# Five hand-ordered engine programs of a linear-attention and MoE layer are written out anew, with another table of PSUM banks

## What is computed

```
x = x + attention(layernorm(x)):   q = elu(x Wq') + 1, k = elu(x Wk') + 1, v = x Wv'  (16 heads of 16)
    out_i = q_i . sum_{j<=i} k_j v_j' / (q_i . sum_{j<=i} k_j + 1e-8), then out Wo'
x = x + ffn(layernorm(x)):         8 experts of 256 -> 128 -> 256 (silu(x Wg) * (x Wu)) Wd, weighted by
    a router (sigmoid, bias, best 2 of 4 groups, best 4 of 8 experts), and one shared expert without weight
```

## Time and profile before

| | |
|---|---|
| median of three runs | 1032.64 us |
| the profiled execution | 1031.95 us, of which its span (first to last instruction) is 1030.2 us |
| PE, DVE busy | 1007.4 us (98%), 838.3 us (81%) |
| POOL, ACT busy | 537.6 us (52%), 422.3 us (41%) |
| DMA | 96.48 MB, 94 GB/s in the mean |

### The profile page before, as it was taken

One profiled execution on the slowest core, in us unless ns is written; L12 is line 12 of the kernel. 1 busy time (PEld: TensorE's weight loads), 2 busy tenths in 40 slices (PEclk: granted clock), 3 DMA queues, 4 the chain that ended last, 5 costly groups with the idle time before them and its releaser, 6 DMA issues.

```text
span 1030.2 us, 22106 instructions
## 1 busy us (share of the span) xinstructions
PE 1007.4 (98%) x8437; PEld 859.6 (83%) x8437; DVE 838.3 (81%) x1776; ACT 422.3 (41%) x750; POOL 537.6 (52%) x440
## 2 busy tenths in 40 slices
PE   6889999999999999999999999999999999999997
PEld 5768888888888888888888888888888888888886
DVE  4888888888978889898788978889888888977554
ACT  5754343434434344343434434344343434422222
POOL 5864545556354463545556345463545556343643
PEclk9999999999999999999999999999999999999999
DMA  5011425345252543425345253444424345231321
GB/s 204 3 47 57 104 63 137 66 117 110 62 144 60 137 83 105 109 58 139 67 114 111 59 142 70 135 83 104 107 64 136 66 121 114 59 107 58 102 82 42
DMA packets 235160, 96.48 MB, mean 94 GB/s; under 512 B 161712, under 2 KB 217520, under 8 KB 235056
## 3 DMA queue, kind: packets, MB, share of 16 engines
q1 hardware_dynamic: 235056, 95.07, 36.1%
HBM read 66.60 MB, written 28.44 MB: 92 GB/s over the span
## 4 chain that ended last, share of the span: by engine, by line
PE 90%; DVE 3%; ACT 2%; DMA 2%; issue 1%; POOL 1%; SPq 0%; DVEq 0%; ACTq 0%; POOLq 0%
PE bank L997 55%; PE y_bank L997 19%; PE bank L1106 6%; PE bank L1122 5%; PE bank L1093 2%; PE bank L1136 2%; PE bank L1148 1%; DMA cw_all<-in_w_qkvo 1%; DMA x_dram<-blocks 0%; DMA cw_all<-cw_dram 0%; DMA expo<-x_dram 0%; ACT wg_hi L580 0%; DVE et L965 0%; DVE x_mid L990 0%; ACT expo L641 0%
## 5 line engine op out<-in xcount | busy, mean ns | idle before, releaser
L997 PE MATMUL bank<-xt_hi,wg_hi 128*128 128x512 f32 x576 | 237.4, 412 | 3.0 <-DVE et L965 2.3
L746 POOL TENSOR_TENSOR h_lo<-et,h_hi 128x512 fp32r<-128x512 f32 x142 | 180.9, 1290 | 96.6 <-ACT h_hi L696 96.4
L997 PE MATMUL bank<-xt_lo,wg_hi 128*128 128x512 f32 x576 | 228.5, 397 | 0.0
L997 PE MATMUL bank<-xt_hi,wg_lo 128*128 128x512 f32 x576 | 228.5, 397 | 0.0
L743 POOL TENSOR_TENSOR et<-et,cw_all 128x512 f32<-128x512 f32 x124 | 163.5, 1339 | 115.1 <-DVE et L971 97.6
L871 DVE TENSOR_TENSOR scores<-bank,cst 128x512 f32<-128x512 f32 x240 | 152.6, 681 | 41.4 <-PE bank L1106 34.1
L997 PE MATMUL y_bank<-wd_hi,h_hi 128*128 128x256 f32 x576 | 165.0, 286 | 0.3 <-POOL h_lo L746 0.3
L997 PE MATMUL y_bank<-wd_hi,h_lo 128*128 128x256 f32 x576 | 161.5, 280 | 0.0
L997 PE MATMUL y_bank<-wd_lo,h_hi 128*128 128x256 f32 x576 | 161.4, 280 | 0.0
L997 PEld LDWEIGHTS bank<-xt_hi,wg_hi 128*128 128x128 f32 x576 | 108.6, 189 | 40.5 <-issue 16.8
L965 DVE SCALAR_TENSOR_TENSOR et<-et,bank 128x512 f32<-128x512 f32 x144 | 95.9, 677 | 48.7 <-ACT et L687 48.6
(11 more groups left out here) (131 smaller groups left out, 1830.5 us busy)
## 6 DMA issues: line engine op xcount, KB each, us to landing
...
```

What stands on the lines that cost most here:

```text
L746: nc.gpsimd.tensor_tensor(h_lo[:, i % HR, :], et[:, i % ET, :], h_hi[:, i % HR, :].bitcast(f32), ALU.subtract).then_inc(h_lo_done, 1)
L997: ins = nc.tensor.matmul(dst, l, r, start=first and n == 0, stop=last and n == 2, skip_group_check=shared)
```

## The change

Every list in `FIRST`, `STEP` and `LAST` is another order of the same parts with the same work; each list is also cut at another place, so that `STEP` begins elsewhere in the cycle. `BANK` has other banks for some parts. ACT's order of pieces is no longer 0 to 9, so those who wait for a high half now look up its place in ACT's list; the first masks wait for the one piece that is staged where they write, where they waited for piece 5; the first `cw_load` waits for pieces 8 and 9, where it waited for 9.

```diff
 STEP = { "PE": """
-        ... values.0.1 values.1.1 down.5.3 inter.0.1 inter.1.1 scores.3.1 gate.0.2 router.0.2 values.2.1
-        values.3.1 gate.1.2 up.0.2 inter.2.1 inter.3.1 gate.2.2 k.0.0 q.0.0 k.1.0 up.2.2 down.6.3 up.1.2
-        q.1.0 down.7.3 down.8.3 scores.0.0 up.4.2 v.1.0 v.0.0 gate.4.2 gate.5.2 state.0.0 ...
+        ... values.0.1 values.1.1 down.3.3 inter.1.1 scores.3.1 gate.0.2 router.0.2 values.2.1 values.3.1
+        gate.1.2 gate.2.2 up.0.2 inter.2.1 down.7.3 inter.3.1 down.6.3 inter.0.1 k.0.0 q.0.0 k.1.0 up.2.2
+        v.1.0 up.1.2 q.1.0 scores.0.0 down.8.3 v.0.0 gate.5.2 gate.3.2 up.3.2 gate.4.2 state.0.0 ...
 FIRST = { "PE": """
-        turn.0.0 turn.1.0 warm.17.0 v.1.0 k.0.0 q.0.0 v.0.0 k.1.0 q.1.0 scores.0.0 k_turn.0.0 scores.1.0
-        warm.8.0 turn.0.1 turn.1.1 ...
+        warm.8.0 turn.1.0 turn.0.0 warm.17.0 k.0.0 q.0.0 v.1.0 k.1.0 q.1.0 v.0.0 scores.0.0 scores.1.0
+        k_turn.0.0 turn.0.1 turn.1.1 ...
     "ACT": """
-        piece.0.0 piece.1.0 turn.1.0 turn.0.0 piece.2.0 v.1.0 piece.3.0 k.0.0 piece.4.0 piece.5.0 q.0.0 ...
+        piece.4.0 piece.1.0 piece.0.0 turn.1.0 turn.0.0 piece.3.0 piece.2.0 k.0.0 q.0.0 piece.5.0 ...
     "SP": """
-        load_x.0.0 consts.0.0 piece.0.0 piece.1.0 piece.2.0 load_x.0.1 piece.3.0 ...
+        load_x.0.0 piece.4.0 piece.1.0 piece.0.0 consts.0.0 piece.2.0 piece.3.0 load_x.0.1 ...
 LAST = { "ACT": """
-        ... gate.3.15 split.2.15 split.3.15 gate.4.15 gate.5.15 ...
+        ... gate.3.15 split.2.15 gate.4.15 gate.5.15 split.3.15 ...
     "SP": """
-        ... cw_store.0.15 cw_load.0.15 cw_load.1.15 cw_load.2.15 store.0.14 cw_load.4.15 cw_load.3.15 ...
+        ... cw_store.0.15 cw_load.2.15 cw_load.0.15 cw_load.5.15 cw_load.1.15 cw_load.7.15 cw_load.6.15
+        cw_load.3.15 store.0.14 cw_load.4.15 store.0.15
 BANK = {
-    ... ("gate", 8): 3, ("router", 0): 1, ("turn", 1): 5, ("up", 8): 5, ...
+    ... ("gate", 8): 5, ("router", 0): 5, ("turn", 1): 1, ("up", 8): 3, ...
@@
-        split_hi = sem("split_hi")
+        split_hi, SPLIT_HI = sem("split_hi"), nth("ACT", ("piece",))
@@ cw_load, on SP
                     if b == 0:
-                        wait_split(sp, NP - 1)
+                        for n in range(NS, NP):
+                            wait_split(sp, n)
@@ mask, on ACT and likewise on DVE
                     if b == 0:
-                        wait_split(act, KC + 3)
+                        wait_split(act, KC + (i % SM) // 2)
@@ piece, on POOL and likewise on DVE
-                    pool.wait_ge(split_hi, i + 1)
+                    pool.wait_ge(split_hi, SPLIT_HI["piece", i, 0])
```

More of the change, by code:

```diff
@@ L40 @@
+        inter.1.1 scores.3.1 gate.0.2 router.0.2 values.2.1 values.3.1 gate.1.2 gate.2.2 up.0.2 inter.2.1
+        down.7.3 inter.3.1 down.6.3 inter.0.1 k.0.0 q.0.0 k.1.0 up.2.2 v.1.0 up.1.2 q.1.0 scores.0.0
+        down.8.3 v.0.0 gate.5.2 gate.3.2 up.3.2 gate.4.2 state.0.0 up.4.2 wo.0.1 up.5.2 wo.1.1 down.0.2
+        scores.1.0 down.1.2 down.2.2 gate.6.2 gate.8.2
         """,
     "ACT": """
-        split.5.3 split.3.3 split.4.3 gate.8.3 gate.7.3 wide.1.1 gate.6.3 ln1_apply.0.0 take.2.2 take.3.2
@@ L51 @@
+        weigh.5.2 weigh.3.2 rstd2.0.1 weigh.4.2 split.3.2
         """,
     "DVE": """
[L53 to L56 removed]
@@ L59 @@
+        den.1.0 at.1.1 state.0.0 gate.4.2 gate.5.2 gate.3.2 up.3.2 up.5.2 up.4.2 wo.1.1 wo.0.1 ln2_stats.0.1
+        mask.4.0 mask.6.0 ln2_apply.0.1 blocks.1.1 mask.5.0 mask.7.0 ln1_stats.0.-1 gate.6.2
         """,
     "SP": """
-        load_x.0.0 put.1.2 get.1.2 put.0.0 get.0.0 cw_store.0.2 cw_load.1.2 cw_load.0.2 put.2.0 get.2.0
-        cw_load.2.2 cw_load.3.2 store.0.3 cw_load.4.2 cw_load.6.2 cw_load.7.2 cw_load.5.2
+        cw_load.7.3 cw_load.6.3 cw_load.5.3 get.1.2 put.0.0 get.0.0 cw_store.0.2 cw_load.1.2 cw_load.0.2
@@ L63 @@
+        put.2.0 cw_load.4.2 get.2.0 store.0.3 cw_load.3.2 cw_load.2.2 load_x.0.-1 put.1.1
         """,
@@ L66 @@
     "PE": """
-        turn.0.0 turn.1.0 warm.17.0 v.1.0 k.0.0 q.0.0 v.0.0 k.1.0 q.1.0 scores.0.0 k_turn.0.0 scores.1.0
-        warm.8.0 turn.0.1 turn.1.1 k_turn.1.0 state.0.0 values.0.0 scores.2.0 inter.0.0 values.1.0 scores.3.0
-        k.0.1 q.0.1 inter.1.0 state.1.0 values.2.0 values.3.0 q.1.1 inter.2.0 scores.0.1 inter.3.0 warm.10.0
-        k.1.1 wo.0.0 wo.1.0 scores.1.1 k_turn.1.1 v.1.1 v.0.1 k_turn.0.1 values.0.1 state.0.1 scores.2.1
-        state.1.1 turn.3.0 inter.0.1 turn.2.0 inter.1.1 values.1.1 scores.3.1 gate.1.0 router.0.0 gate.0.0
@@ new lines @@
+        k.1.1 wo.0.0 wo.1.0 scores.1.1 k_turn.0.1 v.1.1 k_turn.1.1 v.0.1 state.0.1 values.0.1 scores.2.1
+        turn.2.0 inter.1.1 turn.3.0 inter.0.1 values.1.1 state.1.1 warm.10.0 scores.3.1 gate.0.0 gate.1.0
+        turn.1.2 turn.0.2 gate.2.0 router.0.0 values.2.1 values.3.1 inter.3.1 k.0.2 q.0.2 k.1.2 up.0.0
+        inter.2.1 q.1.2 k_turn.0.2 v.1.2 up.1.0 v.0.2 down.0.0 scores.0.2 up.2.0 gate.3.0 gate.4.0 state.0.2
+        k_turn.1.2 gate.5.0 up.4.0 wo.1.1 wo.0.1 up.3.0 up.5.0 down.1.0 scores.1.2 gate.6.0 down.2.0
@@ L136 @@
+        split.7.14 split.8.14 split.6.14 weigh.2.15 weigh.0.15 weigh.1.15 split.0.15 split.1.15 split.2.15
+        weigh.3.15 weigh.4.15 weigh.5.15 split.4.15 split.5.15 split.3.15 split.6.15
         """,
     "DVE": """
[L138 to L140 removed]
@@ L146 @@
-        weigh.6.15 gate.8.15 up.8.15 split.7.15 split.8.15 result.0.15
+        gate.8.13 gate.7.13 state.1.15 up.7.13 up.6.13 up.8.13 mask.11.15 mask.10.15 mask.9.15 mask.8.15
+        mask.12.15 mask.13.15 mask.14.15 mask.15.15 router.0.14 spread.1.15 route.0.14 rank0.0.14 rank1.0.14
+        mult.1.15 gate.0.14 spread.0.15 up.0.14 result.0.13 mult.0.15 gate.2.14 at.1.15 at.0.15 up.2.14
+        gate.3.14 gate.1.14 wo.0.15 up.1.14 wo.1.15 ln2_stats.0.15 up.3.14 ln2_apply.0.15 blocks.1.15
+        gate.4.14 up.4.14 gate.5.14 up.5.14 gate.8.14 gate.6.14 gate.7.14 up.8.14 up.7.14 up.6.14
@@ L147 @@
+        router.0.15 route.0.15 rank0.0.15 rank1.0.15 gate.1.15 gate.0.15 up.0.15 gate.2.15 up.2.15 up.1.15
+        result.0.14 gate.4.15 gate.3.15 up.4.15 up.3.15 gate.5.15 up.5.15 gate.7.15 up.7.15 gate.8.15
+        weigh.7.15 gate.6.15 up.6.15 weigh.6.15 split.7.15 up.8.15 split.8.15 result.0.15
         """,
     "SP": """
-        put.1.14 get.1.14 cw_store.0.14 cw_load.0.14 cw_load.3.14 store.0.13 cw_load.1.14 cw_load.4.14
-        cw_load.2.14 cw_load.5.14 put.1.15 get.1.15 cw_load.6.14 cw_load.7.14 cw_store.0.15 cw_load.0.15
```

158 lines of the change are left out of this document (73 added, 85 removed).

## The result

The changed kernel takes 1055.38 us in the median of four runs (1052.91 to 1057.05) where the kernel before, run beside it, takes 1032.48 (1032.22 to 1032.79): ratio 1.022, 95% interval 1.0199 to 1.024. The forecast was 1028.2, 4.3 us less than the kernel before, with a range up to 1036.0. Measured is 23 us more than before, so both the direction and the range were wrong.

The account below looks back on a forecast made before the run. PE, busy 98% of the span, was taken as the bound, leaving only its waits, matmul-kind changes and low clock to win. 4.3 - 3.5 + 1.5 - 2.6 - 4.1 = -4.4 us gave a 1028.2 median, range 1023.0 to 1036.0.

Parts of the forecast that it names:

- (1): Start: three pieces go ahead of the constants, so PE's first product comes later, +4.3 us (ends +3.0 and +5.5).
- (2): First batch behind the late start runs denser, with the q.1 wait and warm.8 gone: -3.5 us (ends 0 and -6.5).
- (3): PE, whole program: more changes between fp32 and fp32r matmuls, 151 fp32 runs where there were 129: +1.5 us.
- (4): Middle steps: PE's waits, such as at state.0, go: -2.6 us over 13 steps (ends 0 and -4).
- (5): Last batch: PE's 2.35 us wait and the half clock behind it go, every product finds its input: -4.1 us.
- (6): Waits on named pieces and the new banks: 0, since the new waits are met long before.
- A: Rival: scores.0 waits in every step for q_split.0, late on ACT; 0.6 us a step, 1036.0, slower; chance 0.16.
- B: Rival: nothing comes back after the late start, first batch gains 0, constants cost +4.8: 1032.2, no change; chance 0.14.
- D: Rival: the wait at the end only moves, to cw_load.4: 1032.3, no change; chance 0.08.
- C: Rival: the constants are not late, queued transfers being served side by side; start costs +0.4: 1024.3, faster; chance 0.08.
- E: Rival: on PE only changes of the tiling mode cost: 1026.0, faster; chance 0.06.
- the two signs: The forecast is wrong if the constants land at 7.3 us again, or if a middle step is over 62 us.

Follow-up runs that it names:

- b_con3: Kernel before, with SP asking for three pieces ahead of the constants in the start: 1037.03 us, ratio 1.0055.
- a_state: Changed kernel with constants asked for first and, on DVE in the start, state.0 of batch 1 ahead of ln2_apply of batch 0: 1051.64 us, ratio 1.0188.
- b_end: Kernel before, with last router-weight loads ahead of batch 14's store and gate.4, gate.5 ahead of split.3 in the last batch: 1028.63 us, ratio 0.9971.
- b_named: Kernel before, with only the change's waits on named pieces taken over: 1031.43 us, ratio 0.9992.
- a_nocoll_route: Changed kernel with a_state's start edits, and two-SBUF-input operations of rank0 and route replaced by reductions (comparisons and bias left out): 1027.66 us, ratio 0.9967.

## Why the prediction was wrong

**The step that failed** is the one that isn't in the sum: what it costs that DVE's routing moves next to POOL's subtractions. I costed only the order of PE and the named waits, and took every operation of DVE at its length in the trace of before. The move of `rank0` ahead of `gate.0` got no term, though I wrote of the start that "DVE is near its limit there".

| term | forecast | measured |
|---|---|---|
| (1) constants later | +4.3 | +6.2 to the first product in the profiled run, +4.1 to +4.8 in four other runs with the same start, +5.1 in time in b_con3 |
| (2) first batch denser | -3.5 | +1.8, and +3.0 to +3.4 in the four other runs; with the constants first and `state.0` ahead of `ln2_apply` +0.4 in a_state, +1.4 to +2.0 in three others |
| (3) more changes of kind on PE | +1.5 | about 0 |
| (4) middle waits go | -2.6 | -1.5 without collisions (739.85 for 741.36 over twelve steps; 740.68 to 742.83 in b_end, b_named and b_con3), +16.0 with them |
| (5) wait at the end goes | -4.1 | -0.8; -3.3 alone, in b_end; -5.3 in a_nocoll_route |
| (6) named pieces, banks | 0 | 0 in b_named (the banks were not tried alone) |

Against the sum, the start (1, 2) is 7.2 us worse, the twelve steps (3, 4) 17.1 and the end (5) 3.3, together the 27.6 between forecast and profile.

(1) The mechanism was right, and the size within its ends but for the one run: three pieces moved the constants from 7.3 to 12.9, since the engines moved 213 GB/s from 4 to 6 us, 313 from 6 to 8 and 334 to 373 up to 12, and not the 387 that I took. At the mean of these four windows, 308, the 1.57 MB of the forecast take 5.1 us, an estimate that covers most of the 5.6. From PE's start to its first product it then took 8.1 us, near the 7.9 of the forecast, but 6.6 to 7.2 in the four other runs: that these lie within the ends is in part luck, the one error against the other. That the transposes run at half clock, as the forecast has it, is read from their length alone (0.22 us each, later 0.12): the rows give a granted clock of 1.00 there. That the late start would be carried to the end in full b_con3 shows, for the lists before. (2) The wait of 0.98 us at `q.1` did go, and the first `scores` came 8.6 us behind the first product, where it took 10.0 before. But PE stood 1.56 us at 32.32, 0.99 at 52.28 and 2.44 at 67.54 instead, and half clock followed the last. Only that last wait was traced to its cause, and mending it gave 1.3 us; why the rest of the stretch is no shorter than before stays open. (3) Seven of the twelve steps of a_nocoll_route take 61.52 or 61.53 us, with ten runs of fp32 parts, and the shortest before 61.56 with eight. The timeline of the changed kernel shows why:

```profile
840.90 0.38 PE L1140 MATMUL bank<-qf,st 128*128 128x128 f32 x2
841.04 0.36 PE L1001 MATMUL y_bank<-wd_hi,h_hi 128*128 128x256 f32 x1
841.24 0.28 PE L1001 MATMUL y_bank<-wd_lo,h_hi 128*128 128x256 f32 x1
841.36 0.29 PE L1001 MATMUL y_bank<-wd_hi,h_lo 128*128 128x256 f32 x1
```

The first matmul behind `inter.2` holds the next up by 0.20 instead of 0.12 us, as I had it, but itself starts only 0.14 us behind the two fp32 ones: what is lost behind a short fp32 part seems to be gained ahead of it. So the result by the Trainium skill's rule on the tiling mode (TensorEngine Tiling (Array Packing), Key Properties), which made this term -0.7, was nearer than mine. (4) `state.0` had no wait, as forecast. (5) Right for its own wait, and wrong that every product of batch 15 finds its input: the walk left out DVE's `route`, whose operations took up to 1.33 us beside POOL.

**The rivals.** A said a wait in every step, and it came, but at another place and twice as long: ahead of `k.0`, `q.0` and `k.1`, for banks that DVE reads, not for `q_split`. B (nothing comes back after the late start) is what (1) and (2) did, and more. D (a wait at the end only moves) was half right, and named the wrong part. C was wrong, E right about its term. Of the two signs that the forecast named for being wrong, a middle step over 62 us is what the trace of after shows. It was a weak sign, though: four of the twelve steps of the kernel before take 62.11 to 62.18 us.
